# A graph network's edge steps: which tiles come row by row, which by products, and where those products stand

## What is computed

```python
def _gine_layer(x, src, dst, edge_attr, eps, We, be, W1, b1, gamma, beta, W2, b2):
    e = edge_attr @ We + be
    m = jax.nn.relu(x[src] + e)
    agg = jax.ops.segment_sum(m, dst, num_segments=x.shape[0])
    h = ((1.0 + eps) * x + agg) @ W1 + b1
    mu = jnp.mean(h, axis=0)
    var = jnp.mean(jnp.square(h - mu), axis=0)
    h = (h - mu) * jax.lax.rsqrt(var + BN_EPS) * gamma + beta
    h = jax.nn.relu(h)
    return jax.nn.relu(h @ W2 + b2)
```

## Time and profile before

| | |
|---|---|
| three runs | 1920.86, 1928.99, 1932.24 us (median 1928.99) |
| the profiled execution | 1921.04 us, its span 1919.2 us |
| TensorE (PE) busy | 1399.5 us, 73% of the span |
| VectorE (DVE) busy | 1293.6 us, 67% |
| GpSimd (POOL) busy | 978.0 us, 51% |
| ScalarE (ACT) busy | 273.9 us, 14% |
| mean granted clock of TensorE | 0.875 of full speed |
| DMA | 306.84 MB, 160 GB/s over the span |
| gathers by GpSimd from the table, L695 | 972, 945 ns each |
| gathering products, L1711 | 1632 in 490.3 us |
| row loads by SP, L607 | 2560 |

### The profile page before, as it was taken

One profiled execution on the slowest core, in us unless ns is written; L12 is line 12 of the kernel. 1 busy time (PEld: TensorE's weight loads), 2 busy tenths in 40 slices (PEclk: granted clock), 3 DMA queues, 4 the chain that ended last, 5 costly groups with the idle time before them and its releaser, 6 DMA issues.

```text
span 1919.2 us, 25205 instructions
## 1 busy us (share of the span) xinstructions
PE 1399.5 (73%) x7507; PEld 802.4 (42%) x7507; DVE 1293.6 (67%) x2331; ACT 273.9 (14%) x651; POOL 978.0 (51%) x1038
## 2 busy tenths in 40 slices
PE   1568888879658878872955878887295678888648
PEld 0244555445325544441532545454153344545324
DVE  7967778767467776762647768676354867777547
ACT  1200101105101100010510100010050000011004
POOL 4455665560656666661065666556106556666600
PEclk9979988889878989995987999898597889999869
DMA  6556665553655666662265666665226556666613
GB/s 228 160 165 174 170 174 167 155 170 115 203 146 170 178 175 183 172 182 69 87 200 162 177 180 176 169 176 169 62 98 197 169 155 180 175 178 176 181 51 120
DMA packets 105657, 306.84 MB, mean 160 GB/s; under 512 B 21826, under 2 KB 22978, under 8 KB 105516
## 3 DMA queue, kind: packets, MB, share of 16 engines
q0 software_dynamic: 82240, 269.55, 49.2%
q1 hardware_dynamic: 23276, 35.62, 5.8%
HBM read 292.29 MB, written 12.80 MB: 159 GB/s over the span
## 4 chain that ended last, share of the span: by engine, by line
SPq 40%; issue 28%; PE 26%; DVE 5%; DMA 1%; DVEq 0%; ACT 0%
SPq L607 33%; PE y_ps L1860 6%; SPq L601 6%; PE y_ps L1711 6%; PE pair_ps L1664 6%; PE h_ps L1813 3%; DVE rows L1278 1%; PE uT_ps L1766 1%; PE uT_ps L1759 1%; PE uT_ps L1773 1%; DVE rows L1262 0%; PE uT_ps L1748 0%; DVE pair_sb L1205 0%; PE h_ps L1640 0%; PE pair_ps L1799 0%
## 5 line engine op out<-in xcount | busy, mean ns | idle before, releaser
L695 POOL DMA_INDIRECT rows<-node_table,src_fast x972 | 918.6, 945 | 704.0 <-issue 263.0
L1278 DVE SCALAR_TENSOR_TENSOR rows<-We_ps,negw_fast,rows 128x512 f32<-128x512 f32 x1028 | 700.3, 740 | 0.4
L1664 PE MATMUL pair_ps<-rows,onehot 128*32 128x512 f32 x2504 | 415.0, 692 | 309.3 <-DVE rows L1278 196.7
L1711 PE MATMUL y_ps<-table_parts,src_onehot 128*128 128x512 f32 x1632 | 490.3, 438 | 19.0 <-issue 18.0
L1711 PEld LDWEIGHTS y_ps<-table_parts,src_onehot 128*128 128x128 f32 x1632 | 310.1, 204 | 328.9 <-issue 263.9
L1278 DVE SCALAR_TENSOR_TENSOR rows<-We_bc,negw_fast,y_ps 128x512 f32<-128x512 f32 x204 | 151.5, 743 | 312.3 <-remote 176.1
L1664 PEld LDWEIGHTS pair_ps<-rows,onehot 128*32 128x32 f32 x2504 | 60.7, 114 | 437.6 <-issue 243.2
L1813 PE MATMUL h_ps<-uT,W_sb 128*128 128x128 f32 x1152 | 158.0, 297 | 70.2 <-issue 69.9
L1813 PEld LDWEIGHTS h_ps<-uT,W_sb 128*128 128x128 f32 x1152 | 149.9, 211 | 86.7 <-issue 85.8
L847 ACT COPY pair_sb<-pair_ps 128x512 f32<-128x512 f32 x76 | 44.3, 582 | 783.8 <-remote 407.5
L1096 DVE TENSOR_TENSOR src_onehot<-y_ps,src_bc 128x512 fp32r<-128x512 f32 x204 | 138.5, 680 | 0.0
(11 more groups left out here) (201 smaller groups left out, 887.3 us busy)
## 6 DMA issues: line engine op xcount, KB each, us to landing
be_bc<-node_table SPq DMA_DIRECT2D x1536, 2.0 KB
b_bc<-node_table SPq DMA_DIRECT2D x1024, 2.0 KB
rows<-node_table,src_fast POOLq DMA_INDIRECT x972
node_table<-rows SPq DMA_DIRECT2D x29, 256.0 KB, 2.0
x_now<-x_pad SPq DMA_DIRECT2D x10, 512.0 KB, 6.4
W_sb<-W SPq DMA_DIRECT2D x4, 1024.0 KB
rows<-W SPq DMA_DIRECT2D x16, 256.0 KB, 2.7
out<-rows SPq DMA_DIRECT2D x8, 256.0 KB
```

The lines of the kernel that those rows point to most:

```text
L695: nc.gpsimd.indirect_dma_start(rows[:, slot, :], None, source, bass.IndirectOffsetOnAxis(places[:, t:t + 1], 0)).then_inc(landed[q], 16)
L1278: last = nc.vector.scalar_tensor_tensor(rows[:, slot, :], We_of, negw_fast[:, t:t + 1], row, ALU.mult, ALU.max)
L1664: last = nc.tensor.matmul(pair_ps[h][WIN * win:WIN * (win + 1), :], onehot[:, h, tile - h * PAIR, :], rows[:, slot, :], start=t in firsts, ...
L1711: last = nc.tensor.matmul(y_ps[k % 2][:, :], src_onehot[:, first + at, :], table_parts[:, part, at, :], start=(part, at) == PLACES[0], sto ...
```

## The change

`BY_ROW` has three steps (2, 4, 6) and not five, so SP loads three tiles a layer row by row. All steps from 1 to 8 have seven product tiles (quads 0 to 6), 56 a layer in place of 51. In steps 1, 3, 5, 7 and 8 the tile of quad 5, which GpSimd gathered, is now made by products, and that of quad 7, which came row by row, is gathered by GpSimd; in steps 2, 4 and 6 the tile 31 goes from GpSimd to SP. And `gather_shares` stands behind the block products of its place and not ahead of them. `turned_quads` puts tile 31 last in quad 7 in the steps of `BY_ROW`, as before.

```diff
--- before.py
+++ after.py
@@ -84,7 +84,7 @@
     assert all(slot < W2_SLOT for quad in FINAL for slot, _, _ in quad)
     assert len({slot for quad in FINAL for slot, _, _ in quad}) == LAST
 
-    BY_ROW = [1, 3, 5, 7, 8]
+    BY_ROW = [2, 4, 6]
     ROW_TILE = STEP - 1
     AT_ONCE = 16
     ROW_BYTES = 4 * D
@@ -124,7 +124,7 @@
 
 
     def pe_quads(l, i):
-        return () if i not in SORTED else (0, 1, 2, 3, 4, 6) if i in BY_ROW else (0, 1, 2, 3, 4, 5, 6)
+        return tuple(range(USED_RUNS)) if i in SORTED else ()
 
     PE_TILES = [[(i, q) for i in range(BLOCKS) for q in pe_quads(l, i)] for l in range(L)]
     ON_PE = [[{STEPS[i][q][-1][1] for q in pe_quads(l, i)} for i in range(BLOCKS)] for l in range(L)]
@@ -1678,7 +1678,6 @@
                     if l and i == 0 and q < 2:
                         make_early_rows(l, 8 + 2 * q)
                         make_early_rows(l, 9 + 2 * q)
-                    gather_shares(l, QUADS * i + q)
                     if 0 < i:
                         if q == 0:
                             open_block(n - 1, l, i - 1, True)
@@ -1687,6 +1686,7 @@
                             close_block(n - 1, i - 1)
                         if q == (2 if final else 3):
                             product_h(n - 1, l, i - 1)
+                    gather_shares(l, QUADS * i + q)
                     if q == 0 and l == 0 and i == 0:
                         sum_w(0)
                     if q == 1 and l == 0:
```

## The result

The changed kernel took **1823.88 us** (median of 4 runs, 1812.61 to 1833.12), the kernel before in the same session 1925.60 (4 runs, 1920.86 to 1932.24): ratio **0.947**, interval 0.939 to 0.954. The forecast was 1825, in a range of 1786 to 1878. The profiled execution took 1830.82 us, 1828.9 of it the span.

A forecast was written before the change was run, and what follows sets the result against it. The prediction saw SP's row-by-row load queue a whole tile late at the end of layers 1 to 3. From 1921.04 us, -90.3 - 22.7 + 12 + 1 = -100 gave 1821, raised for run spread to 1825 us; range 1786 to 1878.

The forecast's parts named there:

- The signs: What traces should show: no row-buffer waits, step 9 at once, layers 1 to 3 shorter by 30 us, 1,792 products.
- Part 1: Quad 7 of step 8, layers 1 to 3: with three row tiles SP is no longer late; -90.3 us.
- part 2: Row waits of 45.4 us in steps 1 to 7 go, half taken as already caught up; -22.7 us.
- part 3: Twenty more tiles gathered by products in steps 1, 3, 5, 7, 8, at 0.6 us a tile; +12 us.
- Part 4: Gathering products moved behind the block products: taken as 0, bounded by 20 us gain and the third rival's loss.
- the third rival: Gather of quad 5 queued behind `product_h` stalls 32 sorted steps: 122 us more, 1947 us, slower; chance 5%.
- Half (a): Ahead of `product_h`: a full gather and sum cover ScalarE's `uT` copy, cutting TensorE's idle time; at most 20 us gain.
- Part 5: At the start: `src_bc` has 56 columns for 51, one more group of products and one more ScalarE copy; +1 us.
- All waits off: Rival: SP kept the pace of steps 1 to 7, nothing caught up, added products free; -154, 1770 us; chance 12%.
- Every product paid: Rival: TensorE is the bound, so added products cost their full 56 us; -33, 1888 to 1892 us; chance 17%.
- The new queue: Rival: quad 5's gather, queued in order behind `product_h`, stalls 32 sorted steps; 122 us, 1947 us; chance 5%.
- The change doesn't do it: Rival: the wait passes to another row tile, or layers end later for another reason; about 1925 us; chance 4%.

The follow-up runs named there:

- e9: The kernel before, with one row in four of SP's row tiles loaded in two halves; 2222.92 us, ratio 1.1512.
- e10: The changed kernel, with one row in four of SP's row tiles loaded in two halves; 1883.69 us, ratio 0.9724 to the kernel before.
- e11: Row tiles in steps 2, 4, 6 and 8, seven product tiles a step, gathering products ahead of block products as in the kernel before; 1806.27 us, ratio 0.9355.
- 1925 group: The sessions in which the kernel before took about 1925 to 1930 us, including the result's session and those of the profile used for the prediction.
- 1489 group: The two follow-up sessions in which the kernel before took 1488.77 and 1488.86 us.
- e6: The kernel before with SP's reading of row numbers written twice; its instructions stayed those of the kernel before; 1488.36 us, ratio 1.0003.
- e12: The changed kernel, but with the gathering products ahead of `product_h` at that place alone; 1806.31 us, ratio 0.9346 to the kernel before.
- e5: The changed kernel itself, run again where the kernel before takes 1489 us; 1502.59 us, ratio 1.0096 to the kernel before.

## Why the prediction was right, and where not

**The signs.** No message waits for a row buffer, step 9 follows step 8 at once, there are 1,792 gathering products, and `product_h` idles for 24.6 us: four signs came as forecast. Two didn't. Steps 1 to 9 of layers 1 to 3 came 27.9 to 28.4 us shorter, not 30 and more, and those of layer 0 15.4 us shorter, not as long or 3 us longer. Steps of over 41 us, named as a sign of being wrong, are there: steps 1 and 8 of layers 1 to 3 and step 3 of layer 2 took 41.2 to 44.3 us. But step 8 had taken 43.5 to 45.6 before, and the mean of these layers' steps 1 to 8 went only from 39.4 to 39.6.

**Part 1, -90.3.** Right to 0.2 us: step 9 of layers 1 to 3 is 30.5, 30.3 and 29.7 us shorter. e9 and e10 show the mechanism from the other side, and e11, where four tiles are in time. No run takes part 1 alone in the 1925 group, so its size rests on step 9 in the profiles. The tiles had 30 to 58 us in hand in layers 1 to 3, where the prediction had over 40. Its condition is a threshold: SP's pace times its tiles against the time to the last use. In the 1925 group five tiles ended 402 us after the first was begun, where VectorE wanted the last at 373. In the 1489 group (e6, layer 1) they end after 261 us, with no wait. The prediction took SP's pace of one profile as a property of the kernel. In the 1489 group part 1 is worth 0.

**Parts 2 and 3, -22.7 and +12.** The sum of parts 2 to 4 was -10.7, and steps 1 to 8 gave -9.7; but this is no proof of the terms. The kernels that keep the gathers ahead of `product_h` show parts 2 and 3 nearly by themselves: steps 1 to 8 came 27.5 us shorter than before in e12 and 32.3 in e11 (which has one gather fewer a layer), not 10.7. In layer 0 VectorE waited for no row tile before, so nothing of part 2 can be there; part 3 was to cost 3 us, and these steps came 9.2 us shorter in e11 and 11.2 in e12. In layers 1 to 3 the two parts were to give 13.7 and gave 23.1 and 16.3. So part 3 had the wrong sign in layer 0: more tiles by products and fewer by GpSimd made its steps shorter, and VectorE waited less at product tiles (73.6 and 72.7 us for 84.9). This rests on one profile of each kernel, with runs that spread over 10 to 20 us, and why it is so stays open. In layers 1 to 3 nothing tells part 2 from part 3. In the 1489 group the tiles given to TensorE cost 3 us in layer 0, 0.6 a tile as taken, and nothing elsewhere, where GpSimd is the bound; and part 2 is 0 there.

**Part 4, 0.** This is the part that failed. It put the gather of quad 5 at 6.9 us after the sum of quad 3 began and VectorE's need of it at 6.5, and called the 0.4 us between them a little. In the result's own trace the medians over 32 steps are 7.8 us, with single ones up to 12.5, and 6.6, and the wait is 2.9 us in the mean; in e5 they are 6.7 and 4.5 us. So in the 1925 group it was mainly the gather that came late, and in the 1489 group VectorE that came early, both in the place that the third rival named. The time saved at quad 6, which the part set against it, doesn't make up for it: VectorE's waits at quads 5 and 6 are 95.3 us after and 47.8 in e12. Half (a) was seen as forecast, `product_h` idling 24.6 us for 70.2, but that idle time seems to be worth nothing: e11 has 44.1 us of it and e12 16.9, and both took 1806. Measured: about +20 us in the 1925 group, +17.5 to +21.5 in the 1489 group, +7.2 there with the old sets, where three steps in eight have the tile. Two errors of like size and opposite sign (part 4 too cheap, parts 2 and 3 too dear) brought the total to 1 us of the median. That is luck.

**Part 5, +1.** The first `finish_u` came 4.5 us later (96.7 for 92.2). In the 1925 group it lies anywhere from 90.8 (e9) to 98.7 us (e11), in the 1489 group at 82.6 to 83.0 in every kernel, old sets or new: nothing there can be put down to the change.

**The rivals.** *All waits off* (-154) fell by the total: the steps of layers 1 to 3 stayed at 36 to 44 us. *Every product paid* (1888) fell with it. For its ground, the trace of before bears out the rule that the Trainium skill gives in "Perfetto Trace Analysis", section "Tensor Engine Instruction (MATMUL, LD_WEIGHTS)": 116 messages of VectorE waited for a product tile there, and they began 2.3 us after the computed end of the tile's last product in the median, and up to 12.2; in e5, of the 1489 group, 39 such messages began 0.04 us after it, all of them. The trace agrees with the rule, but how late TensorE is belongs to the session, not to the products. *The new queue* was priced at 122 us and given 5%: the mechanism is real, its price was about a sixth of that, and in the 1489 group it does turn the sign, with part 1 worth 0. *The change doesn't do it* is what the 1489 group came nearest to in part 1. The chances hold for runs at the pace of the profile; that the same kernels could run in the 1489 group, where the change is slower, no number of the prediction covers.

## What to carry to other kernels

When the bound is a queue of small issues (128 a tile here), work out its pace times its tiles against the time of the last use, and treat the result as a threshold that another run of the same chip may stand on the other side of: here the same edit is -5.3% in one group and +0.9 to +1.0% in the other. On an engine served in order, put what another engine waits for ahead of a long group that nobody waits for soon, and check the consumer's time at every place, not at the one where the two orders meet. A total that comes out right does not prove its terms: here two errors cancelled, and only the runs that held back one part of the change showed it.

## What the hardware showed that was not expected

- The kernel before took 1489 or 1925 to 1930 us, 30% apart, with nothing between, and chip 12 showed both within some ten minutes. VectorE was busy for 237 us and GpSimd for 202 in layer 1 either way, and the DMA engines moved 206 or 160 GB/s.
- In the 1925 group single instructions of SP's queue take 0.7 us and up to 1.4 us, where the 1489 group has 0.03 (a move) and 0.23 (an issue); VectorE's messages began up to 12.2 us after the computed end of the product that they waited for, where the 1489 group has 0.04 us.
- The granted clock of the kernel before was 0.88 in layer 1 in the 1925 group and 0.97 in the 1489 group: TensorE got less of it where it stood idle more (it was busy for 73% of the layer and for 88%).
- Where the code reads the same sixteen numbers into registers twice, the reading whose values are never used leaves no instruction in the trace (160 readings in e6, as before).
